# First layer and causal attention in one block: the shared expert moved into the routing's tail, and a place of its own for the fourth expert pair's split weights

## The reference: what is computed

```python
x = x + self_attention_0(layernorm(x))             # 16 heads of 16, with biases
x = x + cross_attention_0(layernorm(x), ctx)       # masked, its result layer-normed
x = x + moe_0(layernorm(x))                        # 32 experts, 4 per row, capacity 256, and a shared expert
x = x + causal_attention_1(layernorm(x))
x = x + cross_attention_1(layernorm(x), ctx)       # 16 query heads of 128, 4 key heads, rotary angles
x = x + moe_1(layernorm(x))                        # 64 experts, 8 per row, and a gated shared expert

# inside moe_0
h = rmsnorm(x); scores = softmax(h @ gate); top 4 renormalised
buf[e, pos] = h[token]                             # rows past the capacity are dropped
routed = sum of (silu(g) * u) @ w2 of the slots, weighed
shared = (silu(h @ shared_gate) * (h @ shared_up)) @ shared_down
out = h_in + routed + shared
```

## Time and profile before

| | us |
|---|---|
| median of three runs | 934.87 (929.0 to 935.24) |
| the profiled execution | 933.45 |
| its span, first to last instruction | 931.7 |
| PE busy in it | 806.8 (87%) |
| DVE / ACT / POOL busy | 655.9 / 553.3 / 304.6 |
| mean granted TensorE clock | 0.939 |

### The profile page before, as it was taken

One profiled execution on the slowest core, in us unless ns is written; L12 is line 12 of the kernel. 1 busy time (PEld: TensorE's weight loads), 2 busy tenths in 40 slices (PEclk: granted clock), 3 DMA queues, 4 the chain that ended last, 5 costly groups with the idle time before them and its releaser, 6 DMA issues.

```text
span 931.7 us, 16610 instructions
## 1 busy us (share of the span) xinstructions
PE 806.8 (87%) x5619; PEld 537.7 (58%) x5626; DVE 655.9 (70%) x1388; ACT 553.3 (59%) x1735; POOL 304.6 (33%) x266
## 2 busy tenths in 40 slices
PE   3898887638999388967999999999779999999996
PEld 2677666516888257724677777777434444444443
DVE  2775487847997389638999999896546666666654
ACT  1777775235877257726878877777334444444442
POOL 1111235760000587117555556551022222222220
PEclk9998998559999679979999999999989999999999
DMA  8970001115997321010000000002234444444421
GB/s 296 392 312 2 1 7 42 63 68 187 331 330 265 99 75 52 1 54 1 1 1 1 1 2 1 1 1 75 75 99 124 117 114 122 118 117 116 118 72 46
DMA packets 35888, 90.82 MB, mean 97 GB/s; under 512 B 6502, under 2 KB 9065, under 8 KB 35306
## 3 DMA queue, kind: packets, MB, share of 16 engines
q1 hardware_dynamic: 32746, 81.63, 27.0%
q0 software_dynamic: 3072, 8.30, 2.8%
HBM read 67.71 MB, written 22.29 MB: 97 GB/s over the span
## 4 chain that ended last, share of the span: by engine, by line
PE 46%; DVE 5%; ACT 2%; issue 1%; POOL 1%; DMA 1%; DVEq 0%; SPq 0%; ACTq 0%
PE xpr L1541 9%; PE xps L1541 9%; PE xpr L1439 7%; PE xpt L1556 5%; PE xpo L1556 4%; PE xpo L1486 4%; PE xps L1454 2%; PE xpo L1476 2%; PE xpt L1496 1%; PE xpt L1462 1%; DVE xqr L1746 1%; POOL xsr L1118 1%; DVE xt L1732 1%; DVE xqr L1729 1%; DVE xmx L1751 0%
## 5 line engine op out<-in xcount | busy, mean ns | idle before, releaser
L1133 POOL TENSOR_TENSOR m1ws<-rows,m1ws 128x768 f16<-128x768 f32 x33 | 54.2, 1644 | 201.0 <-ACT rows L1395 171.8
L1273 ACT ACTIVATE xsq<-xt 128x512 f16<-128x512 f32 x66 | 41.5, 629 | 111.2 <-DVE xt L1832 111.2
L1541 PE MATMUL xpr<-red,m1ws 128*128 128x512 f16 x396 | 91.9, 382 | 1.4 <-DVE xt L1832 1.4
L1541 PE MATMUL xps<-red,m1ws 128*128 128x512 f16 x396 | 90.8, 379 | 2.3 <-DVE xt L1832 2.3
L1113 POOL TENSOR_TENSOR xqr<-xqr,xt 128x512 f32<-128x512 f32 x48 | 66.2, 1381 | 53.4 <-DVE xt L1732 53.0
L1836 DVE TENSOR_TENSOR xsq<-xt,xsq 128x512 f16<-128x512 f32 x66 | 45.7, 692 | 41.9 <-ACT xsq L1273 41.7
L1971 POOL DMA_INDIRECT rows<-slots_out,slot x32 | 33.5, 1046 | 109.3 <-DMA slots_out<-m0yo 101.4
L1541 PEld LDWEIGHTS xpr<-red,m1ws 128*128 128x128 f16 x396 | 39.0, 99 | 48.7 <-issue 3.5
L1541 PEld LDWEIGHTS xps<-red,m1ws 128*128 128x128 f16 x396 | 38.7, 98 | 49.0 <-issue 2.7
L1210 ACT ACTIVATE xsq<-xpr 128x128 f32<-128x128 f32 x192 | 50.8, 286 | 16.0 <-PE xpr L1439 15.8
L1556 PE MATMUL xpt<-xsq,m1ws 128*128 128x512 f16 x198 | 49.4, 387 | 6.3 <-DVE xsq L1836 6.3
(11 more groups left out here) (301 smaller groups left out, 2049.5 us busy)
## 6 DMA issues: line engine op xcount, KB each, us to landing
rows<-in_m_w SPq DMA_DIRECT2D x33, 384.0 KB, 4.3
slots_in<-m0h SPq DMA_DIRECT2D x1, 8192.0 KB, 26.6
m0rg<-in_m_wgu SPq DMA_DIRECT2D x16, 512.0 KB, 5.1
m0xg<-slots_in SPq DMA_DIRECT2D x32, 256.0 KB, 4.1
slots_out<-m0yo SPq DMA_DIRECT2D x32, 256.0 KB, 3.6
ang<-wt_dram SPq DMA_DIRECT2D x20, 256.0 KB, 3.9
turns<-wt_dram SPq DMA_DIRECT2D x20, 256.0 KB, 4.1
red<-wt_dram SPq DMA_DIRECT2D x20, 256.0 KB
```

The lines of the kernel that those rows point to most:

```text
L1133: pool.tensor_tensor(ws[:, u, 1, :], raw[:, u, :], ws[:, u, 0, :], ALU.subtract).then_inc(prep_ok, 1)
L1541: ins = pe.matmul(bank, part(u, sw, c, which), hx[:, sh, c, CH * q:CH * q + CH], start=(i == 0), stop=(i == 5))
```

## The change

1. The store `e` and the store `first` are gone: one store `mo` and one block hold stages 1 and 2, so the barrier between them falls away, and of two clearings before stage 3 one is left. Banks are opened once and shared by both (`banks`). Since SBUF cannot be given back in between, stage 2 takes dead tensors of stage 1: split expert weights, rows and activations lie in the weights of the two attentions (`gone`), the loaded slot blocks and the results in `rows.rows` (`got`), the shared expert's activations in `rope.red`.
2. `LATE` is gone: the last tile's four scatters follow the others on POOL at once.
3. The shared expert is cut into methods of `SlotBuffers`, called from the end of stage 1's lists. PE: its first half before the last `places`, the second half and the eight tiles after it. ACT: its silu and its split around the update of `x`, which is cut into two halves of four tiles. DVE: all its steps behind `shares`.
4. DVE makes the angles after the split of the first two experts' weights and ahead of the split of the rows (`x_low(0)`): they lie in buffers that stage 1 still uses.
5. `a1` has other buffers; `V2` lies in `rd` now, and is set to zero after the first tile's `norm_a`, no longer ahead of everything.
6. Stage 3: pair 3 gets a place of its own (`spare`, in the dead tensor `E`), so that `prep_high(3)` waits for no `down`; on ACT it stands before `act_high(3)`, on PE `hidden(6)` stands before `down(4)`; the loop's first period is written out.

The core of the diff:

```diff
-LATE = NT - 1
...
-                if 0 <= n < LATE:
+                if 0 <= n < NT:
                     pool.wait_ge(route.slot_ok, n + 1)
...
                     scatter(NT - 2, 0, 1, 2, 3)
+                    scatter(NT - 1, 0, 1, 2, 3)
...
-                route.update(act)
+                for q in range(NCH):
+                    route.slots.shared_silu(act, q)
+                    route.update(act, q)
+                    route.slots.shared_high_part(act, q)
...
                 route.places(pe, NT - 2)
+                pe.wait_ge(route.low_ok, NT // NCH)
+                route.slots.shared_hidden(pe, 0)
                 route.places(pe, NT - 1)
+                pe.wait_ge(route.low_ok, NT)
+                route.slots.shared_hidden(pe, 1)
+                for n in range(NT):
+                    route.slots.shared_down(pe, n)
...
                 route.shares(dve)
+                for q in range(NCH):
+                    route.slots.shared_times(dve, q)
+                    route.slots.shared_low_part(dve, q)
+                for n in range(NT):
+                    dve.wait_ge(route.x_up, n + 1)
+                    route.slots.shared_add(dve, n)
...
+                    if n == -2:
+                        dve.memset(V2[:, :, :, :, :], 0.0).then_inc(zeroed, 1)
...
+        spare = E.rearrange("p h k -> p (h k)").bitcast(F16)[:, 0:2 * (GU + D)].rearrange("p (s n) -> p s n", s=2)
+        def split_of(p, u):
+            return spare if type(p) is int and p == NR else ws[:, u, :, :]
...
+            for u in range(NR):
+                body(NR + u, u, 1)
+            with eng.Fori(0, NPAIR // NR - 3) as i:
...
-                if p >= NR:
+                if p > NR:
                     act.wait_ge(y_ok, p + 1)
-                act.activation(ws[:, p % NR, 0, :], raw[:, p % NR, :], ACT.Copy, scale=W_UP)
+                act.activation(split_of(p, p % NR)[:, 0, :], raw[:, p % NR, :], ACT.Copy, scale=W_UP)
...
             silu(4, 0)
+            prep_high(3)
             act_high(3, 1)
-            prep_high(3)
             silu(5, 1)
...
+            hidden(6, 3, 0, 0, 0)
             down(4, *early(4))
-            hidden(6, 3, 0, 0, 0)
             down(5, *early(5))
...
+    def shared_silu(self, act, q):
+        act.wait_ge(self.su_ok, q + 1)
+        act.activation(self.ssg[:, q, :], self.p_s[0][:, :], ACT.Silu, scale=1.0 / (H_UP * W_UP)).then_inc(self.ssilu_ok, 1)
+    def shared_high_part(self, act, q):
+        act.wait_ge(self.sact_ok, q + 1)
+        act.activation(self.sap[:, q, 0, :], self.ssg[:, q, :], ACT.Copy).then_inc(self.sah_ok, 1)
...
+    gone = [w_a0[n].rearrange("p c n -> p (c n)") for n in ("wq", "wk", "wv", "wo")] + [w_c0[n].rearrange("p c n -> p (c n)") for n in ("wq", "wk")]
+    got = rows.rows.rearrange("p a b c -> p (a b c)")
...
-            rope.angles(dve)
...
+        g_low(0)
+        g_low(1)
+        rope.angles(dve)
+        x_low(0)
+        x_low(1)
...
-            with first.stack:
+            block = mo.stack.enter_context(nc.Block())
```

More of the change, by code:

```diff
@@ new lines, in shared_hidden @@
+    def shared_hidden(self, pe, q):
+        pe.wait_ge(self.ws_ok, 1)
+        if q >= 1:
+            pe.wait_ge(self.sact_ok, q)
+        for which in range(2):
+            k = 0
+            for c in range(DC):
+                for sw, sh in PASSES:
+                    ins = pe.matmul(self.p_s[which][:, :], self.ws[:, sw, P * (2 * c + which):P * (2 * c + which) + P],
+                                    self.hs[:, sh, c, CH * q:CH * q + CH], start=(k == 0), stop=(k == 5))
+                    k += 1
+        ins.then_inc(self.su_ok, 1)
@@ L2166, in norm, with update @@
         act.activation(self.slots.h2[:, n, :], self.hg[:, n % 2, :], ACT.Copy, scale=self.rr[:, n, 1:2]).then_inc(self.h2_ok, 1)
-    def update(self, act):
+    def update(self, act, q):
         act.wait_ge(self.up_ok, 1)
-        for n in range(NT):
+        for n in range(NT // NCH * q, NT // NCH * (q + 1)):
             xt = self.C["x"][:, n, :]
-            act.activation(xt, xt, ACT.Identity, scale=self.up[:, 0, n:n + 1], bias=self.up[:, 1, n:n + 1])
+            act.activation(xt, xt, ACT.Identity, scale=self.up[:, 0, n:n + 1], bias=self.up[:, 1, n:n + 1]).then_inc(self.x_up, 1)
     def rows(self, act, n):
@@ L2216, in places, with moe_slots @@
         ins.then_inc(self.pos_ok, 1)
-def moe_slots(nc, C, a, rows, bufs, split, wo, w_a1):
+def moe_slots(nc, C, a, rows, bufs, split, wo, w_a0, w_c0, w_a1, e, block, banks):
     x, ident = C["x"], C["ident"]
@@ new lines, in _, with x_high, silu, g_high @@
+    @block.gpsimd
+    def _(pool):
+        for u in range(2):
+            pool.wait_ge(stored[u], 16 * E0 // 2)
+        rows.fetch(pool, 0, 0, 1, 2, 3)
+    @block.scalar
+    def _(act):
+        def x_high(k):
+            act.wait_ge(xt_ok, k + 1)
+            act.activation(xs[k % 2][:, 0, :, :], p_x[k % 2][:, :, :], ACT.Copy, scale=H_UP).then_inc(xh_ok, 1)
+        def silu(k):
+            act.wait_ge(gu_ok, k + 1)
+            act.activation(sg[:, k % 2, :], p_h[k % 2][:, 0, :], ACT.Silu, scale=1.0 / (H_UP * W_UP)).then_inc(silu_ok, 1)
+        def g_high(k):
+            act.wait_ge(gin[k // 2 % NG], 16 * (k // 2 // NG) + 16)
+            act.activation(wg[k % 2][:, 0, :], rg[:, k // 2 % NG, k % 2, :], ACT.Copy, scale=W_UP).then_inc(gh_ok, 1)
+        def y_out(k):
+            act.wait_ge(y_ok, k + 1)
+            if k >= 2:
+                act.wait_ge(stored[k % 2], 16 * (k // 2))
+            act.activation(yo[:, k % 2, :, :], p_y[k % 2][:, :, :], ACT.Copy).then_inc(yo_ok, 1)
+        g_high(0)
+        g_high(1)
+        x_high(0)
+        x_high(1)
+        for k in range(E0):
+            silu(k)
+            if k + 2 < E0:
+                g_high(k + 2)
+                x_high(k + 2)
+            if k >= 1:
+                y_out(k - 1)
+            if k % 3 == 1 and k // 3 < NT:
+                split.high(act, k // 3)
+            if k % 3 == 2 and k // 3 < XH // 2:
+                wo.high(act, k // 3)
+        y_out(E0 - 1)
+        rope.sines(act)
@@ new lines, in _, with turn, hidden, down @@
+    @block.tensor
+    def _(pe):
+        def turn(k):
+            pe.wait_ge(xin[k % NX], 16 * (k // NX) + 16)
+            if k >= 2:
+                pe.wait_ge(xl_ok, k - 1)
+            for c in range(DC):
+                for s in range(ST):
+                    ins = pe.transpose(p_x[k % 2][:, c, P * s:P * s + P], xg[:, k % NX, s, P * c:P * c + P], ident[:, :])
+            ins.then_inc(xt_ok, 1)
+        def hidden(k):
+            u = k % 2
+            pe.wait_ge(xl_ok, k + 1)
+            pe.wait_ge(gl_ok, k + 1)
+            if k >= 2:
+                pe.wait_ge(act_ok, k - 1)
+            for which in range(2):
+                i = 0
+                for c in range(DC):
+                    for sw, sx in PASSES:
+                        ins = pe.matmul(p_h[u][:, which, :], wg[u][:, sw, P * (2 * c + which):P * (2 * c + which) + P],
+                                        xs[u][:, sx, c, :], start=(i == 0), stop=(i == 5))
+                        i += 1
+            ins.then_inc(gu_ok, 1)
+        def down(k):
+            u = k % 2
+            pe.wait_ge(act_ok, k + 1)
+            pe.wait_ge(din[k // 4 % ND], 16 * (k // 4 // ND) + 16)
+            if k >= 2:
+                pe.wait_ge(yo_ok, k - 1)
+            else:
+                pe.wait_ge(sx_ok, NT)
+            for s in range(ST):
+                ins = pe.matmul(p_y[u][:, s, :], ac[:, u, P * s:P * s + P], rd[:, k // 4 % ND, k % 4, :], start=True, stop=True)
+            ins.then_inc(y_ok, 1)
+        turn(0)
+        turn(1)
+        for k in range(E0):
+            hidden(k)
+            if k + 2 < E0:
+                turn(k + 2)
+            if k >= 1:
+                down(k - 1)
+        down(E0 - 1)
```

365 lines of the change are left out of this document (129 added, 236 removed).

## The result

The changed kernel takes 925.2 us (median of 10 runs, 919.99 to 927.82) against 934.21 (10 runs, 929.0 to 936.21): a ratio of 0.9911, interval 0.9884 to 0.9938. Its profiled execution took 923.72 us with a span of 921.9, 9.8 less than the span of before.

What follows compares the result with a forecast made beforehand. PE was taken as the bound in stretches the change leaves alone, with gains where PE stands still. Terms -5.1 + 2.2 - 0.5 + 0.3 - 7.2 = -10.3 against 933.45 gave 923.2, forecast as 924, range 918.5 to 929.5.

Steps and rivals of the forecast that it cites:

- stage 3: Between down(3) and step 7, PE's pause goes since pair 3's split no longer waits: 7.2 us won, ends 5.3 and 7.8.
- The first place: Routing's tail and shared expert, where PE works 4.94 of 17.60 us: an earlier first expert, partly lost to the low clock.
- rival (b): Stage 3: the wait moves to pair 4, PE pauses at step 8, 3.6 us goes back: 927.5; chance 0.11.
- Pair 4's split: Stage 3: it still waits for down(4), is ready at 686.1 against step 8's start at 687.8, 1.7 us to spare.
- The first expert: End of the routing and shared expert: the first expert's matmuls begin at 215.1 in place of 220.22, 5.1 us won.
- The end to the bad: First expert's start: gain of only 3.4 us with both shared-expert halves at the low clock and late places.
- The low clock at the loop's start: Expert loop after a 4.8 us PE pause: half of the slow stretch lost, 2.2 us; nothing if the clock stays up.
- PE is the bound there: Loop over 32 experts: PE is busy 82.28 of 83.80 us, 2.62 us an expert, so PE bounds it.
- One clearing less: Barrier ahead of stage 3: one clearing of two goes, at most half of 1.55 us, 0.5 won.
- The memset: Zeroing of V2 between norm_a(0) and norm_b(0) may hold up POOL's fetches: 0.3 us lost, up to 1.0.
- the second kind: DVE instructions with two SBUF inputs or in a two-port mode, which hold GpSimd's port; claimed the only kind in the trace.
- rival (a): The first place yields next to nothing, as angles and cold loop eat 5.4 us: about -7.5, 926.5; chance 0.22.

Runs made afterwards that it cites:

- e2: The changed kernel with stage 3 as it was before, so the first place alone; 933.0 us, ratio 0.9987 to the kernel before.
- e8: The kernel before with pair 3's own place in stage 3, but the old orders on ACT and PE; 927.4 us, ratio 0.9927.
- e10: The kernel before with 20 unused matmuls filling PE's pause between down(3) and down(4) in stage 3; 930.0 us, ratio 0.9962.
- e4: The changed kernel with 12 unused matmuls in PE's pause ahead of the first expert; 922.6 us, ratio 0.9881 to the kernel before.
- e11: The kernel before with four buffers for the experts' results in place of two; 930.2 us, ratio 0.9962.
- e5: The changed kernel with the angles moved into DVE's wait between the shared expert's halves; 917.2 us, ratio 0.9820 to the kernel before.
- e3: The changed kernel with the angles moved on DVE behind x_low(1); 918.0 us, ratio 0.9840 to the kernel before.

## Why the prediction was right, step by step

The forecast, 924 with a range of 918.5 to 929.5, holds 925.2. How the sum came about is another matter. The forecast's terms make -10.3; in the two traces they make -5.9 + 4.7 + 0.1 - 7.4 = -8.5. The part in stage 3 was right in cause and nearly in size. The first place was forecast at -3.1 (-5.1 + 2.2 - 0.5 + 0.3), and e2 gives -1.2 (-3.2 to 0.7): the forecast lies at the edge of that, and what came out near 924 rests on stage 3.

- **Stage 3: -7.2 forecast, -7.4 seen.** The main mechanism held: the place takes the wait away (e8), the pause of 5.3 goes, and 2.2 more is the clock behind it (e10). Pair 4's split was forecast 1.7 us early and is 1.9 early; rival (b) did not come. One step was wrong: ACT's early split "costs nothing" for ACT, but POOL's part of it held up DVE and cost 0.4 us ahead of `down(3)`; pair 4's does the same to DVE ahead of step 6's `down`, for 0.3. The trace of before showed the like: a DVE product of 0.69 us took 1.68 beside POOL's split (680.82).
- **The first expert: -5.1 forecast, -5.9 seen.** On the scale of before (2.2 us are the earlier start) the second half begins at 196.1 (forecast 196.8), the slots' loads leave at 204.2 (204.1), `x_low(0)` starts at 213.6 (about 214) and the first expert at 214.3 (215.1). All but the slots are 0.4 to 0.8 early: the routing's last step ended at 195.4 on that scale, not at 196.1. Tile 7's `places` began 0.2 later than before, but at the full clock (0.30 and 0.39 us in place of 0.64 and 0.61), and was through earlier. Over more traces the early start is 5.1, as forecast. The end to the bad, 3.4, does not follow from its own terms: with 5.28 for 4.0 and 0.9 for 0.3 it is 3.2.
- **The low clock at the loop's start: +2.2 forecast, 2.7 seen.** The two slow experts lose 1.63 and 1.03 against the full pace (3.39 and 3.64 from one to the next, before 1.76 and 2.61), and e4 gives both back; I had taken a rise after 4.4 us (4.6 by the clock of 0.78 in the earlier trace rows), and it came after about 5.6 (212.1 to some 217.7). The loop is longer by 4.7 in these traces; the other 2.0 are no part of the forecast and lie in the loop's spread.
- **"PE is the bound there", read from 82.28 busy of 83.80 us: wrong.** Before, the 31 steps of the loop could be done in 81.0 us (e11); it took 84.2 to 86.1. ACT and PE before, at one of ACT's waits for a store:

```profile
261.76 0.60 ACT L2312 ACTIVATE m0yo<-m0py 128x512 f32<-128x512 f32 x1 [2.60 <-DMA slots_out<-m0yo]
```

```profile
261.35 1.47 PE L2381 MATMUL m0ph<-m0xs,m0wg 128*128 128x256 f16 x12
262.66 0.60 PE L2368 MATMUL m0px<-ident,m0xg 128*128 128x128 f32 x4
263.66 1.13 PE L2395 MATMUL m0py<-m0rd,m0ac 128*128 128x256 f32 x4 [0.40 <-DVE m0ac L2424]
265.05 1.48 PE L2381 MATMUL m0ph<-m0xs,m0wg 128*128 128x256 f16 x12 [0.26 <-DVE m0xs L2417]
```

  From expert to expert it is 3.70 us in place of 2.61, 1.1 lost, of which 0.66 show as idle; the rest is in groups of matmuls that no longer overlap. The Trainium skill, Perfetto Trace Analysis, section "Identifying the Most-Contended Engine", says that matmul busy share is no good measure of how near PE is to its limit. These runs agree: PE was busy 82.69 of 84.18 us in this loop before, and with four result buffers the same loop took 81.0.
- **One clearing less: -0.5 forecast, nothing seen** (1.57 after, 1.55 before).
- **The memset: +0.3 forecast, +0.1 seen** (15.99 to 16.11). The Trainium skill, SBUF — State Buffer, section "Who interferes with whom", says that a DVE instruction with at most one SBUF input, outside the two-port modes, does not contend with GpSimd. The trace agrees: the fetch beside the memset took 1.00 us, like those around it. The angles, whose first step has two tensor inputs, slowed a scatter to 2.11 in e5. That the trace of before "has only the second kind" was not so: a one-input step of the routing, too (TENSOR_REDUCE, 0.37 us at 191.08), stood beside a scatter, of 0.99.
- **The rest** of the difference between the two executions, -2.2, +0.4, +2.1 and -1.5, lies, but for 0.4 of the +2.1, in code that the change leaves alone, and nearly cancels. That is luck.

So rival (a), "the first place yields next to nothing", was nearer than its 0.22: e2's 0.9987 can't be told from it, and the reason is the one given there, the angles on the chain and the low clock, some 3 us each (e3, e4).

## What to carry to other kernels

A step that a barrier used to hide goes on the chain once the barrier is gone: look for what stood in its shadow (here 3.2 us of angles) and put it where its engine waits for something else. A pause of PE can cost twice, itself and the slow clock behind it (here 2.7 us behind one of 4.3 and 2.2 behind one of 5.3), and the second part can be measured by filling the pause. When work moves, ask what runs beside it at the new place: POOL's split came to stand beside DVE's product and held it up. Before a stretch is called bound by PE, compare its length with the steps at their steady pace, and look at the waits for stores: two buffers in place of four cost 4 us of 85.
